# Graph attention softmax with in-place exponentials ahead of the transposes, and a later quantisation of the bit weights

## The reference

```
p[row, n, h] = exp(score[row, n, h] - max_n score[row, n, h])      # no edge: score = -3e38, p = 0
out[row, h]  = sum_n p[row, n, h] * V[n, h] / sum_n p[row, n, h]
```

## Time and profile before

| | us |
|---|---|
| median of 3 runs | 892.9 |
| lowest, highest | 890.57, 898.55 |
| profiled execution, its own time | 893.61 |
| its span | 891.9 |

### The profile page before, as it was taken

How to read it: one execution, slowest core, us unless ns; L and a number is a source line. 1 busy time by engine, 2 the same in 40 slices (tenths; PEclk the granted TensorE clock), 3 DMA queues, 4 the chain that set the end, 5 groups by cost and what they waited for, 6 DMA issues and landing times.

```text
span 891.9 us, 9443 instructions
## 1 busy us (share of the span) xinstructions
PE 640.9 (72%) x2807; PEld 305.3 (34%) x2807; DVE 540.2 (61%) x1487; ACT 264.7 (30%) x1089; POOL 228.3 (26%) x232
## 2 busy tenths in 40 slices
PE   5952336423318708982779998618999999999997
PEld 2420112201107704441355544313343443344332
DVE  3457998899878995448454234463446854445533
ACT  2104766557541312441113111011222222222222
POOL 5144677777753510000000000010110111011100
PEclk9985557755556958995788999858999999999999
DMA  8598487788749059103000001182999999999991
GB/s 332 218 382 316 139 260 260 245 275 254 249 138 369 32 174 406 56 0 141 1 0 1 0 0 71 67 336 94 409 417 410 410 406 410 415 420 414 417 362 37
DMA packets 46581, 208.27 MB, mean 234 GB/s; under 512 B 7984, under 2 KB 12592, under 8 KB 36928
## 3 DMA queue, kind: packets, MB, share of 16 engines
q1 hardware_dynamic: 27152, 145.70, 41.0%
q0 software_dynamic: 19376, 61.95, 20.6%
HBM read 199.93 MB, written 10.31 MB: 236 GB/s over the span
## 4 chain that ended last, share of the span: by engine, by line
PE 52%; DVE 7%; DMA 2%; ACT 1%; issue 1%; DVEq 0%; POOLq 0%
PE bank L797 14%; PE bank L825 7%; PE bank L817 6%; PE bank L712 4%; PE bank L727 3%; PE bank L533 2%; PE bank L634 2%; PE bank L640 2%; PE bank L786 2%; PE bank L528 2%; DMA R<-tok_tab,slot_tok 2%; PE bank L745 1%; PE bank L742 1%; DVE sm L1090 1%; PE bank L736 1%; PE bank L686 1%
## 5 line engine op out<-in xcount | busy, mean ns | idle before, releaser
L908 ACT ACTIVATE R<-R 128x128 f32<-128x128 f32 x384 | 113.0, 295 | 109.0 <-DVE R L1211 109.0
L577 PE MATMUL bank<-R 128*128 128x384 bf16 x144 | 50.7, 487 | 125.7 <-DVE R L1172 125.7
L797 PE MATMUL bank<-R 128*64 128x512 f32 (+1 forms) x432 | 108.2, 610 | 0.0
L486 POOL DMA_INDIRECT R<-tok_tab,slot_tok x34 | 34.2, 1005 | 280.2 <-DVE slot_f L1567 272.2
L533 PE MATMUL bank<-R,late 128*128 128x512 f32 x168 | 81.1, 644 | 0.7 <-DMA R<-L_Ww 0.7
L1207 DVE TENSOR_TENSOR R<-R 128x1032 f32<-128x1032 f32 x48 | 59.0, 1230 | 26.9 <-DMA R<-tab_src,e_i 14.0
L825 PE MATMUL bank<-R 128*128 128x512 bf16 x306 | 71.9, 380 | 1.0 <-DVE R L1593 1.0
L1579 DVE TENSOR_TENSOR R<-R,bank 128x256 f32<-128x256 f32 x34 | 14.3, 420 | 95.2 <-ACT R L988 95.2
L908 ACT ACTIVATION_READ_ACCUMULATOR R<-R 128x1 f32 x384 | 71.6, 187 | 0.0
L577 PEld LDWEIGHTS bank<-R 128*128 128x128 bf16 x144 | 13.3, 119 | 158.5 <-DVE R L1172 149.3
L446 POOL DMA_INDIRECT score<-late,e_i x48 | 57.5, 1198 | 30.8 <-DVE late L1166 15.7
(11 more groups left out here) (343 smaller groups left out, 1146.4 us busy)
## 6 DMA issues: line engine op xcount, KB each, us to landing
R<-L_w SPq DMA_DIRECT2D x54, 1536.0 KB, 10.6
late<-L_w SPq DMA_DIRECT2D x18, 1536.0 KB, 9.3
R<-L_w SPq DMA_DIRECT2D x2, 3072.0 KB, 15.0
score<-R POOLq DMA_DIRECT2D x9, 512.0 KB, 13.1
R<-score SPq DMA_DIRECT2D x3, 1536.0 KB, 10.2
R<-L_Ww SPq DMA_DIRECT2D x2, 2048.0 KB, 12.9
R<-L_W SPq DMA_DIRECT2D x4, 1024.0 KB, 9.1
tab_src<-R SPq DMA_DIRECT2D x3, 516.0 KB, 2.7
```

Source lines behind the costliest of these rows:

```text
L577: last = pe.matmul(pb[s][:, 0:N], oh[:, e % 2, 0, P * s:P * s + P], oh[:, e % 2, 1, :], start=(e == 0), stop=(e == ET - 1))
L797: last = pe.matmul(pb[4 + i % 2][part, :], xeT[i % 2][:, k, part], w13[e % NWB][:, k, :], start=(k == 0), stop=(k == KD - 1), tile_positio ...
L908: act_.activation(own, own, ACT.Copy, accum_out=w_e3[:, t, h:h + 1]).then_inc(S("heads_summed"), 1)
```

## The change

Five edits, of which the last two rename or merge semaphores.

1. **Softmax.** DVE no longer adds the negated maximum to `mt`; `row_max` ends at L1244. ACT runs one exponential per tile and head, in place on `mt[i][:, :, h]` (384 elements, 32 bytes apart), with the negated maximum as bias: 24 instructions instead of 18. PE then transposes probabilities. A unit is now (tile, half of the heads, column chunk), ordered by half first; the banks that the transposes go into are 0, 1, 4, 5, 0, 1 in tile 0 and 0, 1, 0, 1, 0, 1 after it. The 18 copies from PSUM to `pT` are split: ACT takes units 3 to 5 and 15 to 17, DVE the other twelve.
2. **Order of the copies.** DVE: maxima of tiles 0 and 1, copies 0 to 2, maxima of tile 2, copies 6 to 8, 9 to 11, 12 to 14. ACT: exponentials of tile 0, copies 3 to 5, exponentials of tiles 1 and 2, copies 15 to 17. PE runs two units of transposes ahead of `attend`.
3. **POOL.** The quantisation moves behind the additions L474.
4. `xg_cleared` is gone: each clearing waits on POOL's own step semaphore.
5. `most_ready` becomes a second count of `over_ready`; `rest_coded` is folded into `rest_named`.

```diff
@@ gpsimd
+            pool.wait_ge(S("shifter_in_ready"), 1)
+            for t in range(NT):
+                pool.tensor_tensor(out=x3[:, t, :], in0=x3[:, t, :], in1=xn3[:, t, :], op=ALU.add).then_inc(S("shifter_added"), 1)
             pool.wait_ge(S("half_sc_ready"), 1)
             half_sc = V_("half_sc", 4)
             for j, w in enumerate((wu, wd)):
...
-            pool.wait_ge(S("shifter_in_ready"), 1)
-            for t in range(NT):
-                pool.tensor_tensor(out=x3[:, t, :], in0=x3[:, t, :], in1=xn3[:, t, :], op=ALU.add).then_inc(S("shifter_added"), 1)
@@ helpers
+        turned_in = (0, 1, 4, 5, 0, 1) + (0, 1, 0, 1, 0, 1) * 2
+        def unit(u):
+            return u // 6, u // 3 % 2, u % 3
+        def by_act(u):
+            return unit(u)[:2] in ((0, 1), (NT - 1, 1))
@@ tensor
+            def transpose_probs(u):
+                i, half, c = unit(u)
+                pe.wait_ge(S("exp_ready"), H * i + 4 * half + 4)
+                sharing = [w for w in range(u) if turned_in[w] == turned_in[u]]
+                if sharing:
+                    pe.wait_ge(*probs(sharing[-1]))
+                for j in range(4):
+                    last = pe.transpose(pb[turned_in[u]][:, P * j:P * j + P], mt[i][:, P * c:P * c + P, 4 * half + j], ident[:, :])
+                last.then_inc(S("probsT_psum"), 1)
...
             for i in range(NT):
-                for c in range(NT):
-                    transpose_scores(i, c)
-                    if c:
-                        attend(i, c - 1)
-                attend(i, NT - 1)
+                for v in range(6):
+                    transpose_probs(6 * i + v)
+                    if v >= 2:
+                        attend(6 * i + v - 2)
+                attend(6 * i + 4)
+                attend(6 * i + 5)
@@ scalar
-            for u in range(2 * NT * NT):
-                act_.wait_ge(S("scoresT_psum"), u + 1)
-                act_.activation(pT[u], pb[u % 2][:, :], ACT.Exp).then_inc(S("probs_ready"), 1)
+            for i in range(NT):
+                act_.wait_ge(S("row_max_ready"), i + 1)
+                for h in range(H):
+                    act_.activation(mt[i][:, :, h], mt[i][:, :, h], ACT.Exp, bias=V_("nmax", 24)[:, H * i + h:H * i + h + 1]).then_inc(S("exp_ready"), 1)
+                for u in range(6 * i, 6 * i + 6):
+                    if by_act(u):
+                        take_probs(u)
@@ vector
-                one(ts(m, m, NEG_FLOOR, -1.0, ALU.max, ALU.mult))
-                for c in range(NT):
-                    part = mt[i][:, P * c:P * c + P, :]
-                    tt(part, part, bc(m[:, None, :], [P, P, H]), ALU.add).then_inc(S("shifted_ready"), 1)
+                ts(m, m, NEG_FLOOR, -1.0, ALU.max, ALU.mult).then_inc(S("row_max_ready"), 1)
+
+            def take_probs(i, half):
+                for u in range(6 * i + 3 * half, 6 * i + 3 * half + 3):
+                    dve.wait_ge(S("probsT_psum"), u + 1)
+                    dve.tensor_copy(pT[u], pb[turned_in[u]][:, :]).then_inc(S("probs_dve"), 1)
...
             row_max(1)
+            take_probs(0, 0)
             row_max(2)
+            take_probs(1, 0)
+            take_probs(1, 1)
+            take_probs(2, 0)
```

More of the change, by code:

```diff
@@ L262, in rest @@
         def rest(eng, one_expert, before=None, after=None):
-            eng.wait_ge(S("most_ready"), 1)
+            eng.wait_ge(S("over_ready"), 2)
             fullest = eng.value_load(most[0:1, 0:1], min_val=0, max_val=N)
@@ L274, in rest, with probs @@
                     after()
+        turned_in = (0, 1, 4, 5, 0, 1) + (0, 1, 0, 1, 0, 1) * 2
[3 more added lines that the diff above has]
+            return unit(u)[:2] in ((0, 1), (NT - 1, 1))
+        def probs(u):
+            return (S("probs_act") if by_act(u) else S("probs_dve"),
+                    sum(1 for w in range(u + 1) if by_act(w) == by_act(u)))
         block = ctx.enter_context(nc.Block())
@@ L470, in _ @@
                 pool.tensor_tensor(out=q, in0=q, in1=w, op=ALU.subtract).then_inc(S("wq_ready"), 1)
-            pool.wait_ge(S("shifter_in_ready"), 1)
-            for t in range(NT):
-                pool.tensor_tensor(out=x3[:, t, :], in0=x3[:, t, :], in1=xn3[:, t, :], op=ALU.add).then_inc(S("shifter_added"), 1)
             pool.wait_ge(S("x_ready"), NT * 6)
             for j in range(NXG):
-                pool.memset(xg[j], 0.0).then_inc(S("xg_cleared"), 1)
+                step(pool.memset(xg[j], 0.0))
             pool.wait_ge(S("tokens_stored"), 16 * (NT + 1))
-            pool.wait_ge(S("xg_cleared"), NXG)
             def gather_tokens(i):
@@ L591, in _ @@
             pe.wait_ge(S("V_ready"), NT)
[L593 to L601, removed]
@@ L603, in attend @@
-            def attend(i, c):
-                pe.wait_ge(S("probs_ready"), 2 * (NT * i + c) + 2)
+            def transpose_probs(u):
[7 more added lines that the diff above has]
+                last.then_inc(S("probsT_psum"), 1)
@@ L606, in attend @@
+            def attend(u):
+                i, half, c = unit(u)
+                pe.wait_ge(*probs(u))
                 if i == NT - 1 and c == 0:
                     pe.wait_ge(S("half_sc_ready"), 1)
-                for h in range(H):
-                    last = pe.matmul(pb[2 + 2 * i + h // 4][:, HV * (h % 4):HV * (h % 4) + HV], pT[2 * (NT * i + c) + h // 4][:, P * (h % 4):P * (h % 4) + P],
-                                     V[c][:, h, :], start=(c == 0 and h % 4 == 0), stop=(c == NT - 1), skip_group_check=True)
@@ L611, in attend @@
-                if c == NT - 1:
+                for j in range(4):
+                    last = pe.matmul(pb[2 + 2 * i + half][:, HV * j:HV * j + HV], pT[u][:, P * j:P * j + P],
+                                     V[c][:, 4 * half + j, :], start=(c == 0 and j == 0), stop=(c == NT - 1), skip_group_check=True)
+                if half == 1 and c == NT - 1:
                     last.then_inc(S("attended_psum"), 1)
             for i in range(NT):
-                for c in range(NT):
-                    transpose_scores(i, c)
-                    if c:
-                        attend(i, c - 1)
@@ L908, in _, with take_probs @@
                     act_.activation(own, own, ACT.Copy, accum_out=w_e3[:, t, h:h + 1]).then_inc(S("heads_summed"), 1)
-            for u in range(2 * NT * NT):
-                act_.wait_ge(S("scoresT_psum"), u + 1)
-                act_.activation(pT[u], pb[u % 2][:, :], ACT.Exp).then_inc(S("probs_ready"), 1)
+            def take_probs(u):
+                act_.wait_ge(S("probsT_psum"), u + 1)
+                act_.activation(pT[u], pb[turned_in[u]][:, :], ACT.Copy).then_inc(S("probs_act"), 1)
+            for i in range(NT):
[5 more added lines that the diff above has]
+                        take_probs(u)
             for t in range(NT):
@@ L1623, in choose_overfull @@
                 one(dve.tensor_reduce(V_("most", 1), V_("beyond", E3), AX, ALU.max))
-                dve.tensor_copy(most[:, :], V_("most", 1)).then_inc(S("most_ready"), 1)
+                dve.tensor_copy(most[:, :], V_("most", 1)).then_inc(S("over_ready"), 1)
             def place_overfull(t):
@@ L1691, in gate_rest @@
                 dve.tensor_copy(rest_tok, rest_rec[:, 0:1]).then_inc(S("rest_named"), 1)
-                dve.wait_ge(S("rest_named"), nth_)
-                ts(rest_code, rest_tok, -float(TOK), None, ALU.add).then_inc(S("rest_coded"), 1)
-                dve.wait_ge(S("rest_coded"), nth_)
+                dve.wait_ge(S("rest_named"), 2 * nth_ - 1)
+                ts(rest_code, rest_tok, -float(TOK), None, ALU.add).then_inc(S("rest_named"), 1)
+                dve.wait_ge(S("rest_named"), 2 * nth_)
                 ts(rest_oh, iota_m[:, :], rest_code, rest_rec[:, 2:3].bitcast(f32), ALU.is_equal, ALU.mult).then_inc(S("rest_spread"), 1)
```

## The result

The changed kernel takes 907.4 us in the median of four runs (904.84 to 909.8), the kernel before 892.1 beside it: ratio 1.016, 95% interval 1.011 to 1.021. It is slower by about 15 us; I had said 893.0, with a range of 886.5 to 899. The profiled execution took 909.8, its span is 908.0.

A forecast was written before the change was run, and what follows sets the result against it. Behind the softmax one DVE chain bounds the kernel while PE idles; DVE, then PE and ACT, set the softmax's end. 893.6 - 5.5 (softmax) + 5.1 (quantisation) = 893.2, stated as 893.0 us, range 886.5 to 899.

The forecast's parts named there:

- The step that failed: Softmax, PE: prices per unit of 0.58 us for transposes and 0.48 for products, read from merged rows.
- the mark that I forecast: Softmax: DVE's start on dividing tile 2, expected to move from 309.74 to 304.2, -5.5 us.
- and lose 4 us: Softmax, ACT: tile 1's exponentials are queued behind copies of units 3 to 5 and lose 4 us.
- The exponentials: Softmax, ACT: 0.87 us per strided head, 6.2 us a tile; bounds 3.9 and 8.4 us a tile.
- -7.3 instead of -5.5: Softmax rival: exponentials at the contiguous price, 0.585 us each, saving 7.3 us instead of 5.5; 891.4 us, 20%.
- The rival of dear exponentials: Softmax, ACT: at 1.1 us apiece nothing is saved (898.7), at 1.6 the kernel is slower by over 1%; 6%.
- The quantisation: Shifter: POOL's moved instructions hold up DVE's chain of tiny operations, +5.1 us; bounds nothing to 9.0.
- The rival of the full lock: Shifter: each POOL instruction shuts DVE out for its whole length, chain +15.6 us; 903.7 us, 8%.
- POOL misses DVE: Shifter rival: POOL's instructions mostly miss DVE's work or DVE wins, +1 instead of +5.1; 889.1 us, 17%.
- The rest: SP's later loads (323.66 to about 346) stay covered; clearings and merged semaphores cost nothing.

The follow-up runs named there:

- filled_both: Changed kernel plus identity transposes on PE into an unused bank, 12 ahead of unit 0 and 11 ahead of unit 6, before the waits for exponentials; ratio 1.008.
- after: Trace of the changed kernel itself, all five edits against the kernel before; 907.4 us median, ratio 1.016.
- before: Trace of the kernel before the change, unmodified; 892.1 us measured beside the changed kernel.
- quant_back: Changed kernel with POOL's quantisation put back ahead of the additions, new softmax kept; ratio 1.009 to the kernel before.
- head_major: Changed kernel with exponentials and transposes taking each head's 384 elements contiguously, which computes wrong probabilities; ratio 1.010 to the kernel before.
- quant_only: Kernel before with only the quantisation moved behind the additions, old softmax kept; ratio 1.003.
- filled_ahead: Changed kernel plus 11 identity transposes on PE ahead of its wait for tile 1's exponentials; ratio 1.016 to the kernel before.
- filled: Changed kernel plus 11 identity transposes on PE at unit 6, placed behind its wait for tile 1's exponentials; ratio 1.010 to the kernel before.
- after_again: The changed kernel run once more, unmodified, for a second trace; 921.6 us against 907.2 for the kernel before on that chip.
- stride_probe: Changed kernel plus six ACT copies of 384 elements at various strides on scratch, ahead of the first exponentials; one run, softmax 47.2 us.
- exps_alone: Changed kernel with units 3 to 5 copied by DVE instead of ACT, so no copies stand between ACT's exponentials; ratio 1.014 to the kernel before.
- best_new: exps_alone plus the quantisation behind layer norm 3 and identity transposes ahead of units 0 (14) and 8 (16); ratio 1.000 to the kernel before.
- old_late: Kernel before, softmax untouched, with the quantisation moved behind the additions and layer norm 3; 890.3 us against 893.4, ratio 0.996.
- old_gap: old_late with PE made to wait for all three shifted pieces of tile 1 before its first transposes; ratio 0.997 to the kernel before.

## Why the prediction was wrong

**The step that failed** is "A unit's transposes take 0.58 us (8 in 1.16), its products 0.48 (16 in 1.90)". The 16 instructions of that row are not four units but two: a float32 product is two matmul instructions here (144 of L609 for 18 units of 4 heads), a transpose is one. A unit's products take 0.95 to 1.0 us alone, and a whole unit follows the one before every 1.33 us at full clock (285.06, 286.38, 287.71 in the rows above), where I had 1.06. PE has 18 x 1.33 = 24 us of work, 5 us more than by my prices, and starts on it at the first maximum + 8.3 us (+ 5.9 before), since it waits for four exponentials and not for one shifted piece. Even with no wait and a full clock throughout, that is 32.2; I had 31.7. `filled_both`, at full clock from 3 us behind unit 0, has 37.9: in the 5.7 us more are its first transposes at the lower clock, the identity transposes, and four waits of some 0.4 us for copies and exponentials.

**The larger part was missing**: the clock, a term that I had at nothing. Of the 14.2 us between the mark that I forecast (31.7) and the measured one (45.9), 8.0 are the clock's by `filled_both`. The other 6.2 are left at full clock, and the wrong price of the products can account for at most 5 of them. I took the clock as full throughout. The new order makes PE wait twice: 5 us ahead of unit 0 (3.1 before) and 1.55 ahead of unit 6. The kernel before waits too, 2.11 us ahead of tile 2, but its clock was back after 3.4 us. I saw the second wait's cause (the exponentials of tile 1 are queued behind ACT's copies, "and lose 4 us") and priced it as time on ACT alone. Behind the second wait PE ran at the lower clock for 20 us. The Trainium skill ("TensorE: Matmul & The Clock Gate", "HAM oscillation — how this bites in real kernels") has waits that take the clock down again in every round of a loop. The traces agree with the fall, behind waits of 1.55 us (`after`) and 2.11 us (`before`). I had not weighed it against this change, and should have.

**The exponentials**: right in kind, a little small. 0.87 forecast, 0.984 measured, a tile 7.2 instead of 6.2 us. The pair `quant_back` and `head_major` puts the whole step to contiguous exponentials at 1.5 us of the mark, where I had 1.8 (-7.3 instead of -5.5). In `filled_both`, at full clock, PE waits 0.38 and 0.40 us for them in tile 1. The rival of dear exponentials is not what happened: they stayed under 1.1 us.

**The quantisation**: right in place and mechanism, and the size nearly. The chain lost 6.1 against 5.1, mostly because a comparison can hold DVE a second time at its end (0.7 us in L487, 0.7 in the second L486), which I had not. A further part that I had at nothing is the second subtraction, which does meet the layer norm: 1.8 of the 2.3 us that the stretch to the first aggregation lost; the rest is the projection's slower start. The chain took 1 us more than I had, and so the layer norm fell beside L488. The rival of the full lock is refuted for comparisons (DVE's operations in between took their normal 0.17) and holds for the subtraction (2.11 us for a cast beside its 2.16). "POOL misses DVE" is refuted.

**The rest**: SP's loads came 31 us later (354.9) without any wait of PE for them, the clearings and merged semaphores cost nothing; right. The stretch behind the first aggregation came out 1.6 us shorter, which I don't explain.

In terms of the runs, the softmax's +8.7 is -4.3 (POOL gone from beside it: 37.2 to 32.9 in `quant_only`), +5.0 (later start and the new order, nearly all at full clock: 32.9 to 37.9 in `filled_both`) and +8.0 (the clock: 37.9 to 45.9). These are differences of single traces. With 6.1 and 2.3 for the quantisation that makes 17; 15 were measured in the medians and 16 in the spans.

**Open**: what decides how long the clock stays down behind an idle stretch. In the new order it took 2.7 us once and 19 another time from nearly the same start (`after`, `filled_ahead`), and 6 or 20 us behind the same gap (`filled`, `after`). In the four traces of the old order it was back within 3.3 to 5.5 us. All six traces with a wait of 1.55 us or more inside the softmax (`before`, `after`, `after_again`, `stride_probe`, `filled`, `exps_alone`) have the lower clock behind it; `filled_both`, `best_new`, `quant_only`, `old_late` and `old_gap`, with no wait over 0.66, keep the full clock to the end once it has risen. Why it comes back in 3 us in some traces and in 20 in others no run shows.

## What to carry to other kernels

Before taking a per-item price from a merged row, divide its instruction count by the program's own count of the line: a row of 16 may be two units or four. And take the step from one start to the next, since neighbouring groups overlap (1.33 us a unit, not 0.65 + 1.00). When a change makes TensorE wait for a new producer, price the wait at both clock levels for everything behind it, and if the wait can't be closed, cover it with idle transposes (8.0 us back for 23 of them, in one trace). Work on GpSimd is not free where VectorE works on SBUF: here it cost next to nothing where VectorE took reciprocals and evacuated PSUM (`old_late`: 17.7 us for the first GCN stretch instead of 17.5).

## What the hardware showed that I had not expected

- ScalarE pays for distance, not for direction: 384 float32 elements 16 or 32 bytes apart take 0.88 to 0.90 us instead of 0.51, whether read, written or both; 8 bytes apart 0.54. The exponential with a pointer bias follows: 0.984 against 0.602.
- TensorE transposes the strided operand at nearly the contiguous price: four take 0.65 us in the new kernel and 0.61 in `head_major`.
- A comparison on GpSimd (one input, 128 x 1024) shut VectorE out for 0.9 us of its 2.86 at the start, and some of them again for 0.7 at the end, in place or not; a subtraction of two inputs held a cast of VectorE for 2.11 of its 2.16 us.
- The clock of TensorE can stay at the lower level for 20 us in which it is busy 20.35 of 20.50 us; in `filled_ahead` it did so for nearly 19 us without a wait.
